# Node numbers of a segment sum: one run into one partition, turned by TensorE, in place of three numbers to each partition

## The reference, cut to what matters

```python
def _L0_gnn_ref(x, edge_attr, u, W1, b1, W2, b2, edge_index):
    recv_idx = edge_index[1]                      # sorted: dst comes in ascending order
    recv_agg = jax.ops.segment_sum(edge_attr, recv_idx, num_segments=n)   # the collection
    ...
    h = jax.nn.relu(collected @ W1 + b1)
    updated_nodes = h @ W2 + b2
    return updated_nodes
...
x = _layernorm(x + _L0_gnn_ref(x, edge_attr_128, ...), axis=-1)
x = _layernorm(x + _L1_gnn_ref(x, edge_index, edge_weight, ...), axis=-1)
```

## Time and profile before

| | |
|---|---|
| median of 3 runs | 3176.68 us (3169.33 to 3176.99) |
| the profiled execution | 3179.64 us, of which span 3177.9 us |
| collection stage | from about 39 to 327 us of the span |
| busy over the span | PE 67%, DVE 65%, POOL 60%, ACT 36% |
| edge rows, `acc<-in_edge_attr`, on SP's queue | 344 loads, 192 KB each, 3.4 us to landing |
| node numbers, `c_node<-drec`, on ACT's queue | 344 loads, 1.5 KB each |
| adds, L448 | 344, 281 ns each |
| matmuls, L486 | 2064 records (six to a body), 393 ns each |

### The profile page before, as it was taken

How to read it: one execution, slowest core, us unless ns; L and a number is a source line. 1 busy time by engine, 2 the same in 40 slices (tenths; PEclk the granted TensorE clock), 3 DMA queues, 4 the chain that set the end, 5 groups by cost and what they waited for, 6 DMA issues and landing times. The chain is left out here.

```text
span 3177.9 us, 60089 instructions
## 1 busy us (share of the span) xinstructions
PE 2140.8 (67%) x13048; PEld 1784.0 (56%) x13049; DVE 2054.2 (65%) x5492; ACT 1130.5 (36%) x3527; POOL 1920.8 (60%) x2110
## 2 busy tenths in 40 slices
PE   4556999975676677667767675666666666667650
PEld 3434899964565565556656543555555555555540
DVE  5555222235777777777777675677777777777666
ACT  1000344422344343344444431343344444443343
POOL 3600111127777777777777335777777777777727
PEclk6665899985667767776776686667777777786765
DMA  7889211124444444444444514444444444444432
GB/s 214 225 250 271 83 36 39 37 78 130 129 122 130 128 128 121 128 130 128 128 123 123 54 52 121 130 131 123 126 129 130 127 121 126 130 130 124 109 33 74
DMA packets 276093, 385.16 MB, mean 121 GB/s; under 512 B 121804, under 2 KB 207772, under 8 KB 275676
## 3 DMA queue, kind: packets, MB, share of 16 engines
q0 software_dynamic: 80768, 220.05, 25.1%
q1 hardware_dynamic: 145628, 163.04, 16.5%
q10 hardware_dynamic: 49536, 0.55, 0.9%
HBM read 360.42 MB, written 23.02 MB: 121 GB/s over the span
## 5 line engine op out<-in xcount | busy, mean ns | idle before, releaser
L1326 POOL DMA_INDIRECT wide<-kv,a_source x1664 | 1679.1, 1009 | 536.3 <-issue 470.3
L1357 PE MATMUL psum<-wide 128*128 128x136 f32 x3328 | 743.0, 380 | 316.7 <-DVE acc L1555 312.0
L1346 PE MATMUL psum<-wide,a_hot_t 128*128 x3328 | 692.1, 372 | 245.8 <-DVE wide L1474 140.4
L1357 PEld LDWEIGHTS psum<-wide 128*128 128x128 f32 x3328 | 627.7, 269 | 409.5 <-DVE acc L1555 321.1
L1346 PEld LDWEIGHTS psum<-wide,a_hot_t 128*128 128x128 f32 x3328 | 595.8, 266 | 314.9 <-issue 308.0
L1555 DVE TENSOR_TENSOR acc<-acc,psum 128x136 f32 x1664 | 488.9, 294 | 303.9 <-issue 124.5
L1413 ACT ACTIVATE a_edge_q<-psum 128x16 f32<-128x16 f32 x416 | 76.6, 184 | 1356.8 <-PE psum L1357 451.8
L1421 ACT ACTIVATE wide<-iota_n,a_spot 128x128 f32<-128x128 f32 x1664 | 526.7, 391 | 29.9 <-PE psum L1357 16.6
L1474 DVE TENSOR_TENSOR wide<-psum,wide 128x512 f32<-128x512 f32 x416 | 286.2, 688 | 290.0 <-DMA wide<-kv,a_source 277.8
L1425 ACT ACTIVATE wide<-wide,ones 128x512 f32<-128x512 f32 x416 | 300.3, 722 | 13.5
L1477 DVE TENSOR_REDUCE a_score<-wide 128x16 f32<-128x512 f32 x416 | 286.4, 688 | 14.3
(11 more groups left out here) (254 smaller groups left out, 2054.6 us busy)
## 6 DMA issues: line engine op xcount, KB each, us to landing
acc<-in_edge_attr SPq DMA_DIRECT2D x344, 192.0 KB, 3.4
a_place<-places SPq DMA_DIRECT2D x104, 512.0 KB, 4.1
wide<-kv,a_source POOLq DMA_INDIRECT x1664, 2.8
kv<-acc SPq DMA_DIRECT2D x49, 128.0 KB, 1.7
kv<-p_pairs SPq DMA_DIRECT2D x49, 128.0 KB
c_node<-drec ACTq DMA_DIRECT2D x344, 1.5 KB
a_cut<-breaks SPq DMA_DIRECT2D x208, 8.1 KB
acc<-in_x SPq DMA_DIRECT2D x49, 64.0 KB, 1.8
```

Source lines behind the costliest of these rows:

```text
L1326: pool.indirect_dma_start(out=ring[:, at.b, n, :], out_offset=None, in_=kv[:, :], in_offset=bass.IndirectOffsetOnAxis(ap=source[at.b][:, n ...
L1346: last = pe.matmul(query_out(q)[:, t, :], hot_t[:, q * QUAD + t, :], queries_of(m, held[q % 2 * QUAD + t]), start=True, stop=True, skip_gr ...
L1357: last = pe.matmul(sum_out(q, t), hot[q % 2][:, t, :], ring[:, (at.b + back) % 2, q * QUAD + t, LEAD:KV], start=True, stop=True, skip_grou ...
```

## The change

A body's 384 node numbers are now loaded as one run into one partition of `nodes` (one piece of 1.5 KB; a half's four bodies take four partitions). TensorE turns them: for each of the three slices one matmul has 4 x 128 node numbers as its weights (every third number of the run) and a 4 x 4 identity as what moves, and gives 128 x 4 numbers in PSUM (`turn_nodes`). The result lies in the back half of bank 2, whose front part holds the sums of the bodies with k % 4 = 2. VectorE's mark reads it from there and waits for the new semaphore `noded`. ACT's loads wait for `noded` too, in place of `away_there`.

TensorE turns the numbers of a half one round ahead, at k = 2 and k = 6, just before that body's matmuls. Since bank 2 must not be read then, TensorE first waits until the mark of the next half has read it (`away_there`), which stands on VectorE behind the add of k = 0 or k = 4. Both halves of round 0 are turned ahead of the rounds, ahead of `move`. The last round turns nothing.

```diff
-        node = sb("node", [P, 2, PART, BT])
+        nodes = sb("nodes", [PART, 2, BE])
...
+        def node_out(g):
+            at = (2 + g) * P
+            return bank[PART // 2][:, at:at + BT * PART].rearrange("p (t b) -> p t b", b=PART)
...
-                    act.wait_ge(away_there, at.value(2, g + 1))
-                act.dma_start(node[:, g, b, :], m["drec"][bass.ds(at.edges[k], BE)].rearrange("(p t) -> p t", t=BT)
+                    act.wait_ge(noded, at.value(2, g + 1))
+                act.dma_start(nodes[b:b + 1, g, :], m["drec"][bass.ds(at.edges[k], BE)].rearrange("(a e) -> a e", a=1)
                               ).then_inc(node_in[g], 16)
...
-                dve.wait_ge(node_in[g], at.value(16 * PART, 16 * PART * (1 + h // 2)))
+                dve.wait_ge(noded, at.value(2, h + 3))
                 dve.scalar_tensor_tensor(away_of[:, g, :, :], repeat(windows_of.unsqueeze(2), 2, BT), -float(WN),
-                                         node[:, g, :, :], ALU.mult, ALU.add).then_inc(away_there, 1)
+                                         node_out(g).rearrange("p t b -> p b t"), ALU.mult, ALU.add).then_inc(away_there, 1)
...
+            dve.wait_ge(noded, 4)
             mark(Round(dve, dve.snap(last_round(dve, m) * 0)), 0)
...
+            def turn_nodes(g):
+                of_tile = nodes[:, g, :].rearrange("b (e t) -> b t e", t=BT)
+                for t in range(BT):
+                    last = pe.matmul(node_out(g)[:, t, :], of_tile[:, t, :], ident[0:PART, 0:PART], start=True, stop=True,
+                                     skip_group_check=True)
+                last.then_inc(noded, 1)
+
             def step(at, k, left):
+                g = k // PART
+                if k % PART == PART // 2:
+                    pe.wait_ge(added, at.body(k + 1 + NS - DEEP))
+                    if left >= PART:
+                        pe.wait_ge(away_there, at.value(2, g + 4))
+                    if left == NS:
+                        pe.wait_ge(node_in[g], at.value(16 * PART, 2 * 16 * PART))
+                        turn_nodes(g)
...
+            pe.sem_inc(noded, 2)
+            for g in (0, 1):
+                pe.wait_ge(node_in[g], 16 * PART)
+                turn_nodes(g)
             rounds(pe, m, step, None, last_round, ((0, move), (8, turn), (11, find_ends), (16, turn_spots)))
```

More of the change, by code:

```diff
@@ L271, in collect_stage @@
         (away_there, hot, summed, added, cleared, coded, moves_ps, taken, turned, fielded, ends_ps, ends, cut, shaped,
-         filled_out, lists_out, spotted, spots_ps) = (sem(n) for n in (
+         filled_out, lists_out, spotted, spots_ps, noded) = (sem(n) for n in (
             "away_there", "hot", "summed", "added", "cleared", "coded", "moves_ps", "taken", "turned", "fielded", "ends_ps",
-            "ends", "cut", "shaped", "filled_out", "lists_out", "spotted", "spots_ps"))
+            "ends", "cut", "shaped", "filled_out", "lists_out", "spotted", "spots_ps", "noded"))
         block = inner.enter_context(nc.Block())
```

## The result

The changed kernel takes 3274.20 us in the median of 4 runs (3269.93 to 3274.84); the kernel before took 3175.88 in the 4 runs beside them. The ratio is 1.031, with a 95% interval of 1.029 to 1.033: slower by 98 us, where 3268 was predicted. The profiled execution has a span of 3272.0 us, 94.1 more than the span before.

The account below looks back on a forecast made before the run. The prediction took VectorE's chain of adds and marks to bound the collection, with TensorE hidden behind it. Turnings +97.4, short waits -7.8, other stalls -4, start +6 gave +92 us, 3268 us, in a range from 3205 to 3305.

Parts of the forecast that it names:

- add to TensorE: Path from a half's first add through the mark's subtraction to TensorE's start on the turning: 0.46 us.
- T: Length of one turning on TensorE, three matmuls in six records: 1.30 us, with ends at 0.74 and 1.68.
- body to third add: From the third body's first record on TensorE to its add on VectorE: 0.80 us.
- 84 turnings: Two turnings in each of 42 rounds, each making its half 1.16 us longer: +97.4 us.
- start, beyond a turning: Round 0's loads, turning and `move` delay round 1's loads and mark 2: +6 us beyond the 1.16 counted.
- node waits and other stalls: In the collection, VectorE's 16 short node waits vanish, -7.8 us; other stalls change by -4, between -15 and +5.
- L955's 0.22 a record: Sixteen TensorE records with 128-column weights take 3.48 us at clock 0.50, giving 1.30 for a turning's six.
- 2.4 GHz: Rival: added TensorE records keep the clock up, T 0.74, sum +45 us, 3221; chance 0.08.
- Cheap loads: Rival: turning's weight loads cost the page's 0.107 us estimate, T 0.64, sum +37 us, 3213; chance 0.08.
- A dearer turning: Rival: no load overlaps the matmul ahead of it, T 1.68, 32 us more, 3300; chance 0.10.
- Faster: Rival: DMA bounds the collection and the turning is hidden (T under 0.14): 3146, or 3155 for node waits only; chance 0.05.
- Come back as waits of TensorE: VectorE's four long node waits, about 14 us, caused on ACT and the queues, move to TensorE: nothing gained.

Follow-up runs that it names:

- the four runs of the table: Changed kernel with nothing turned inside the rounds, 3183.72 us; with transposes for the turning's matmuls, 3206.16; as it is, 3274.20; with each turning done twice, 3378.79.
- the move to another place: Changed kernel with the same turning matmuls moved to the front of the next half (bank 0): 3198.58 us, ratio 1.0084 to the kernel before.
- the loads alone: Kernel before with node numbers loaded as one run, nothing turned, the mark reading zeros: 3162.29 us against 3171.68, ratio 0.9972.
- the shortest turning: Changed kernel with three transposes in place of the turning's three matmuls, at the same place: 3206.16 us, ratio 1.0106 to the kernel before.
- the wait alone: Changed kernel with all its waits but nothing turned inside the rounds: 3183.72 us, ratio 1.0037 to the kernel before.
- the run with later takes: Kernel before with ScalarE's three takes of the move's results each one round later: 3168.01 us, ratio 0.9992.
- the transposes in the same place: Changed kernel with the turning as transposes and at the front of the next half: 3172.01 us against 3171.05 for the kernel before, ratio 1.0008.
- the last kernel: Run loads, transposes at the front of the next half, takes one round later, `move` ahead of the first turning: 3166.06 us against 3171.05, ratio 0.9982.

## Why the prediction was right

**The mechanism.** The idle stretch before the third add, ended by TensorE, the six records right behind the mark, the clock at 0.50, the DMA share well below 0.94 and the vanished waits of VectorE are all there. The mark's subtraction takes 0.17 us from PSUM, as it did from SBUF: that part costs nothing, as predicted. That the turning's length on this path is the cause, and not the loads, the wait or TensorE's load, is shown by the four runs of the table and by the move to another place.

**The sum, term by term.**

| term | predicted | measured |
|---|---|---|
| add to TensorE | 0.46 | 0.52 (219.05 to 219.57), 0.43 (222.75 to 223.18) |
| T | 1.30 | 1.37 |
| body to third add | 0.80 | 0.82 |
| half longer by, mean | 1.16 | 1.275 |
| 84 turnings | +97.4 | +107.1 |
| start, beyond a turning | +6 | +6.7 (8.0 at mark 2, less 1.28) |
| node waits and other stalls | -11.8 | -14.1 (mark 2 to 83: 89.2, less 81 x 1.275) |
| behind mark 83 | 0 | -0.9 (98.8 less 97.2 and two turnings) |
| later stages | 0 | -4.7 |
| sum | +92 | +94 in the spans, +98 in the medians |

T came out at the row with the like matmuls (1.37) and not at L955's 0.22 a record that the prediction preferred: the nearer row in form was the better one. The 0.07 there, 0.02 in the body and in the mean 0.02 in the handing over make the largest term 10 us too small; stalls that went beyond what was put down (2.3), the last halves (0.9) and the later stages (4.7) made up for most of it. These offsets were not forecast: that 92 came as near to 94 as it did is in part luck. One row was read a little too wide: of the 22.0 us of waits, 0.81 stand at mark 84, behind the stretch that they were set against.

**The rivals.** *2.4 GHz* fell: 0.50 throughout. *Cheap loads* fell with T. The Trainium skill ("TensorE: Matmul & The Clock Gate", section "LDWEIGHTS (loading the stationary operand)") gives 128 columns over 1.2 in ns, an estimate of 0.107 us, for each load. The trace has 1.37 / 6 = 0.23 from load to load, so for these matmuls of 32-bit numbers at this clock the measurement decides against the page. *A dearer turning* (1.68) was on the wrong side of 1.37. *Faster* fell in both its parts: the loads alone were worth 9 us and not 22 to 31, and its condition, T under 0.14, is not met by any kernel that turns in this place (the shortest turning, 0.44, still cost 0.41 a half). Even the wait alone, with T at 0, made a half 0.15 longer, so the condition itself was too mild. The 37 us that the prediction gives for the page's T come to 36 by its own terms.

**The long waits.** "Come back as waits of TensorE" was right, though of the 21.5 us only 10.3 are theirs: the three waits ahead of marks 18, 24 and 34, the places of three of the four long waits before. At the place of the fourth, mark 42, no wait for node numbers is left: behind it TensorE waits 5.8 us for edge rows, where before an add waited 4.32 for them on top of the 3.90. Their cause was named as ACT and the queues. Three of four are the takes on ACT, as the run with later takes shows; the fourth lies where the lists go out on SP's queue, and that these make it was not tried.

## What to carry to other kernels

A step on an engine that has time to spare is paid by the path that it makes, not by how busy the engine is: count from the last thing that it waits for to the next thing that waits for it, and set that against what ran there before. The same six records cost 98 us between the second and third body and 27 us at the front of the next half, and half as many and shorter records at that place left every regular half as it was. DMA engines that were busy for 0.94 of a stage, and waited for in 22 us of it, gave 9 us when one queue's eleven hundredths were taken away.

## What was not expected

- The weight loads of the transposes, of 4 x 128 numbers, follow each other at 0.15 us (0.44 for three), those of the matmuls at 0.23 (1.37 for six), at mostly the lower clock; half the records, and each shorter, make the transpose a third of the matmul.
- TensorE was busy for 97.00 of 100 us with matmuls of the turning and of the bodies, and the granted clock was 0.50 all the while. With the transposes in the same place it was busy for less and the clock was higher, at shorter halves:

```profile
210.00:310.00 100.00, 84.77 (x960) 51.91 (x957) 59.99 (x211) 0.00 (x0) 0.00 (x0) 0.59 0.90 283
```

  With nothing turned (the loads alone), at these same distances of the marks, it was busy for 68.96 and the clock was 0.63. What in these orders makes the difference was not tried.
- Some instructions of VectorE lasted about as long as one of GpSimd on a long row of one partition beside them, 2.09 us in place of 0.2 to 0.5 (shown above). In the last kernel it is the one-hot, 0.56 us elsewhere:

```profile
139.62 2.06 POOL L342 TENSOR_TENSOR c_apart<-skip 1x896 f32<-1x896 f32 x1
...
140.02 2.08 DVE L443 TENSOR_TENSOR acc<-iota_n,c_away_of 128x384 f32<-128x384 f32 x1
```

  Not every pair that runs at the same time does it (in the kernel before the one-hot at 137.20 kept its 0.56 beside a GpSimd instruction of 2.48 that began 0.01 after it, while in the two pairs shown GpSimd began first, by 0.06 and 0.40); that the two engines share something is argued from these lines, not shown.
